# Rotated tiles turned by TensorE in transpose mode, preparation in smaller pieces, node sums on TensorE in the lead

## The reference

```
x = x + 0.5 * ffn(layernorm(x))      # 8 experts, threshold routing with capacity 1024
x = x + attention(layernorm(x))      # 16 heads of width 16, 4 nodes for each head
x = x + 0.5 * ffn(layernorm(x))
```

```
q, k, v = x @ Wq, x @ Wk, x @ Wv                    # 16 heads
node_probs = softmax(x @ Wr)                        # over the 4 nodes of each head
pos = clip(cumsum(node_probs, sequence) - node_probs, 0, 2047)
cos, sin = linear interpolation of the rotary tables at pos
cos_w, sin_w = sum over the nodes of node_probs * cos, node_probs * sin
q_r, k_r = q * cos_w + rotate_half(q) * sin_w, the same for k
scores = q_r @ k_r.T / 4 + log(node_probs @ node_probs.T + 1e-8), causal
out = softmax(scores) @ v, then @ Wo
```

## Time and profile before

| | us |
|---|---|
| median of three runs | 2959.88 |
| profiled execution | 2933.87 |
| its span | 2931.7 |
| TensorE matmul busy | 2448.4 (84%) |
| VectorE busy | 1713.1 (58%) |
| ScalarE busy | 1674.4 (57%) |
| GpSimd busy | 990.4 (34%) |

### The profile page before, as it was taken

One profiled execution on the slowest core, in us unless ns is written; L12 is line 12 of the kernel. 1 busy time (PEld: TensorE's weight loads), 2 busy tenths in 40 slices (PEclk: granted clock), 3 DMA queues, 4 the chain that ended last, 5 costly groups with the idle time before them and its releaser, 6 DMA issues. The chain is left out here.

```text
span 2931.7 us, 104032 instructions
## 1 busy us (share of the span) xinstructions
PE 2448.4 (84%) x45962; PEld 1906.9 (65%) x45964; DVE 1713.1 (58%) x3589; ACT 1674.4 (57%) x2102; POOL 990.4 (34%) x1423
## 2 busy tenths in 40 slices
PE   7287645577899999899999989999989999972875
PEld 4155412366688887778888768888778888741554
DVE  6733168888576568766566786666675111177331
ACT  6022123356677777667777767777766777560221
POOL 1078710244232224422222442322243222110787
PEclk9598866799999999999999999999999999985988
DMA  6455511121211112212112222111222111161555
GB/s 230 136 97 104 77 39 30 48 62 40 64 52 57 52 46 79 65 50 60 53 52 56 77 62 57 57 53 56 65 66 61 47 47 47 55 230 22 103 100 75
DMA packets 185107, 207.26 MB, mean 71 GB/s; under 512 B 35984, under 2 KB 151712, under 8 KB 184480
## 3 DMA queue, kind: packets, MB, share of 16 engines
q1 hardware_dynamic: 158880, 165.60, 19.0%
q0 software_dynamic: 24576, 34.10, 7.4%
q10 hardware_dynamic: 1152, 0.26, 0.0%
HBM read 131.68 MB, written 76.02 MB: 71 GB/s over the span
## 5 line engine op out<-in xcount | busy, mean ns | idle before, releaser
L1620 PEld LDWEIGHTS at_mix<-at_val,at_ew 128*64 128x64 f32 x34816 | 1223.5, 138 | 240.7 <-issue 36.1
L1204 ACT ACTIVATE at_ew<-at_ring 128x1024 f32<-128x1024 f32 (+1 forms) x1280 | 1125.2, 898 | 361.1 <-PE at_ring L1602 355.1
L1620 PE MATMUL at_mix<-at_val,at_ew 128*64 128x68 f32 x34816 | 1262.7, 224 | 45.0 <-DVE at_mixed L1466 30.1
L1602 PE MATMUL at_ring<-at_qT,at_kT 98*64 98x512 bf16 (+3 forms) x5120 | 698.7, 352 | 55.7 <-ACT at_ew L1204 36.2
L1125 POOL TENSOR_SCALAR_AFFINE_SELECT at_ew<-at_ew 128x256 f32<-128x256 f32 x512 | 292.6, 576 | 1078.2 <-ACT at_ew L1204 1077.2
L1466 DVE TENSOR_TENSOR at_mixed<-at_mix,at_prob 128x272 f32<-128x272 f32 x256 | 112.3, 439 | 437.1 <-PE at_mix L1620 435.7
L1602 PEld LDWEIGHTS at_ring<-at_qT,at_kT 98*64 98x64 bf16 x5120 | 228.7, 111 | 109.1 <-ACT at_ew L1204 48.3
L1147 POOL TENSOR_TENSOR at_val<-at_vo,at_val 128x256 f32<-128x256 f32 x384 | 266.6, 715 | 7.5
L328 POOL DMA_INDIRECT out_dram<-ffn_xn,ffn_idx_all x128 | 212.9, 1663 | 53.2 <-issue 34.1
L318 POOL DMA_INDIRECT ffn_xn<-table,ffn_idx_all x128 | 123.2, 963 | 311.8 <-DMA ffn_idx_all<-ffn_idx_hi 273.5
L1685 PE MATMUL at_side<-at_w_all,at_turned 128*64 128x512 f32 (+1 forms) x1024 | 203.2, 542 | 13.8 <-DVE at_bounded L1459 5.2
(11 more groups left out here) (224 smaller groups left out, 2759.8 us busy)
## 6 DMA issues: line engine op xcount, KB each, us to landing
table<-ffn_xn SPq DMA_DIRECT2D x32, 512.0 KB, 6.2
q_parts<-at_parts SPq DMA_DIRECT2D x64, 192.0 KB, 2.4
k_parts<-at_parts SPq DMA_DIRECT2D x64, 192.0 KB, 3.0
at_qT<-q_parts SPq DMA_DIRECT2D x128, 96.0 KB
at_kT<-k_parts SPq DMA_DIRECT2D x64, 192.0 KB
ffn_front<-in_L_attn_x_dram SPq DMA_DIRECT2D x16, 512.0 KB, 5.1
ffn_w_in<-in_L_ffn_w_dram SPq DMA_DIRECT2D x32, 256.0 KB, 3.6
at_xin<-out_dram SPq DMA_DIRECT2D x32, 256.0 KB, 5.9
```

What stands on the lines that cost most here:

```text
L1204: act.activation(ew[u % NE_BUF][:, a:b], ring[u % 2][:, a:b], ACT.Exp).then_inc(s["exp_ready"], 1)
L1602: lastm = pe.matmul(ring[u % 2][h:h + HALF, at:at + (CH - t) * P], kT[q][:, kc + j * P + h:kc + j * P + h + HALF], qT[q][:, qc + t * P:qc ...
L1620: m = pe.matmul(mix[block_of[u] % 2][h:h + HALF, t * K * VW:(t + 1) * K * VW], ew[u % NE_BUF][:, col + h:col + h + HALF], val[q][:, tile0 ...
```

## The change

- `turn_rotated` issues 8 matmuls of full width with `is_transpose=True` in place of 16 of half width.
- VectorE's steps are cut in smaller ones: `rotate` leaves its last two operations to `join_halves`; `positions` is split into `positions`, `whole_positions` and `first_angles`; `angles` gives its first two operations to `count_turns`; `node_products` is two steps. In a turn these stand at units of their own, each with its sums behind it, and `normalise` moves from unit 33 to 37 in long turns.
- ScalarE's `next_rsqrt` moves from unit 20 to 16 in short turns (29 to 25 in long ones), `trig` from 16 to 17 and `low_part` from 18 to 19 in short ones.
- In the lead VectorE shifts the logits and takes the softmax ahead of turn weights and rotation. For pairs 0 to 3 it doesn't sum the node products: TensorE does, in `sum_nodes` between `project_values` and `project_qk`, into `ring[0]`, and `turn_weights` reads the sums there. ScalarE's order in the lead stays.
- In the feed-forward programs several semaphores become counts of two common ones, and the residual copy counts on `rows_stored`, for which GpSimd waits ahead of its first gather.

```diff
-                pool.wait_ge(rows_stored, 16 * G + 16)
+                pool.wait_ge(rows_stored, 16 * G + (32 if residual else 16))
                 gather(0)
                 gather(1)
-                if residual:
-                    pool.wait_ge(residual_copied, 16)
...
-                SHORT_AT = (3, 6, None, 8, 9, 12, 15, 18, 16, 23, 20)
-                LONG_AT = (4, 6, 10, 8, 16, 18, 20, 23, BURST + 2, BURST + 4, BURST + 3)
+                SHORT_AT = (3, 6, None, 8, 9, 12, 15, 19, 17, 23, 16)
+                LONG_AT = (4, 6, 10, 8, 16, 18, 20, 23, BURST + 2, BURST + 4, BURST - 1)
...
-                def turn_weights():
+                def turn_weights(early=None):
+                    summed_nodes = sums[:, :, :]
+                    if early is not None:
+                        dve.wait_ge(s["sums_ps"], early + 1)
+                        summed_nodes = ring[0][:, :].rearrange("p (c n) -> p c n", c=4)
...
                 def lead(new, fin):
-                    if fin is not None:
-                        turn_weights()
-                        rotate(fin)
                     shift_logits(new)
                     node_softmax(new)
+                    if fin is not None:
+                        turn_weights(fin)
+                        rotate(fin)
+                        join_halves()
                     positions(new)
+                    whole_positions()
+                    first_angles(new)
                     statistics(new + 1)
+                    count_turns()
                     angles(new)
...
-                    node_products(new)
-                    node_sums(0)
-                    node_sums(2)
-
-                SHORT_AT = (0, 1, 6, 8, None, 10, 12, 13, 14, 18, 19, 20, 21, 23)
-                LONG_AT = (1, 2, 5, 8, 10, 14, 17, 20, 22, 30, 32, 25, 34, 33)
+                    for n in (0, 2):
+                        node_products(new, n, new < LEAD - 1)
+                    if new == LEAD - 1:
+                        for n in (0, 2):
+                            node_sums(n)
...
+                        if at == 1:
+                            turn_weights()
+                        if at == 2:
+                            rotate(fin)
+                        if at == (3 if short else 4):
+                            join_halves()
+                        if at == (14 if short else 20):
+                            largest_squares(fin)
+                        if at == (20 if short else 25):
+                            bound(fin)
...
+                        if at == (12 if short else 17):
+                            count_turns()
+                        if at == (13 if short else 18):
+                            angles(new)
+                        if at == (18 if short else 30):
+                            node_products(new, 0)
+                        if at == (19 if short else 32):
+                            node_sums(0)
+                        if at == (21 if short else 33):
+                            node_products(new, 2)
+                        if at == (22 if short else 35):
+                            node_sums(2)
+                    if more:
+                        if at == (15 if short else 22):
+                            statistics(new + 1)
+                        if at == (23 if short else 37):
+                            normalise(new + 1)
...
-                                    for h in range(0, P, HALF):
-                                        at = (g * 4 + n) * P + h
-                                        lastm = pe.matmul(side[h:h + HALF, n * GP + g * P:n * GP + (g + 1) * P],
-                                                          qkr[:, at:at + HALF], ident[:, :],
-                                                          start=(n % 2 == 0 and g == 0), stop=False, skip_group_check=True)
+                                    at = (g * 4 + n) * P
+                                    lastm = pe.matmul(side[:, n * GP + g * P:n * GP + (g + 1) * P], qkr[:, at:at + P], ident[:, :],
+                                                      is_transpose=True, start=(n % 2 == 0 and g == 0), stop=False, skip_group_check=True)
...
+                    turn_inputs()
+                    project_values()
+                    if fin is not None:
+                        sum_nodes(fin)
+                    for step in (project_qk, sums_before, turn_rotated, take_high_off, take_middle_off, turn_squares):
                         step()
+
+                def sum_nodes(t):
+
+                    pe.wait_ge(s["prods_ready"], t * 2 + 2)
+                    for n in range(2):
+                        each = prods[:, 2 * n:2 * n + 2, :].rearrange("p c (n k) -> p c n k", k=K)
+                        for k in range(K):
+                            lastm = pe.matmul(ring[0][:, n * 512:(n + 1) * 512], ident[:, :], each[:, :, :, k],
+                                              start=(k == 0), stop=(k == K - 1))
+                    lastm.then_inc(s["sums_ps"], 1)
```

More of the change, by code:

```diff
@@ L260, in _ @@
                 if residual:
-                    sp.dma_start(dst, src).then_inc(residual_copied, 16)
+                    sp.dma_start(dst, src).then_inc(rows_stored, 16)
                 def move_idx(e):
@@ L624, in _ @@
                 logits(G - 1)
-                pe.wait_ge(logits_ready, 1)
+                pe.wait_ge(act_stage, LOGITS_COPIED)
                 for t in range(GT):
@@ L1552, in unit @@
-                    if step == 3 and new is not None:
-                        node_softmax(new)
-                    if step == 4 and post is not None:
-                        add_residual(post, 0, 1)
-                    if step == 5 and new is not None:
-                        positions(new)
-                    if step == 6 and new is not None:
-                        angles(new)
-                    if step == 7 and fin is not None:
-                        largest_squares(fin)
-                    if step == 8 and more:
-                        statistics(new + 1)
@@ L1564, in unit @@
-                    if step == 9 and new is not None:
-                        node_products(new)
-                    if step == 10 and new is not None:
-                        node_sums(0)
-                    if step == 11 and fin is not None:
-                        bound(fin)
-                    if step == 12 and new is not None:
-                        node_sums(2)
-                    if step == 13 and more:
-                        normalise(new + 1)
+                    if fin is not None:
[9 more added lines that the diff above has]
+                            bound(fin)
```

86 lines of the change are left out of this document (47 added, 39 removed).

## The result

The changed kernel takes 3013.98 us, the median of four runs (3011.38 to 3017.36), beside 2960.14 us for the kernel before on the same chip: a ratio of 1.0186, 95% interval 1.0171 to 1.0200, or 54 us more. The prediction was 2961 us with a range of 2940 to 2988. It was wrong, and outside its range.

A forecast was written before the change was run, and what follows sets the result against it. TensorE was taken to bound the body, VectorE's chain the lead, and queue order the short turns. Terms +20.6 - 14.7 - 10.0 + 5.0 = +0.9 us on 2959.9 gave 2961 us, range 2940 to 2988.

The forecast's parts named there:

- The lead: Iterations before the first scores: node sums moved from VectorE to TensorE lengthen them, +20.6 us, bounds 15 and 48.
- The queue: Lead iteration: exponential behind the copy of qk, VectorE waiting for it before rotating; 38.6 us instead of 34.2.
- the 6.9 us for the 8 added matmuls: Lead, sum_nodes on TensorE: eight f32 matmuls at 0.86 us each, priced from contiguous reads.
- twice as long: Lead: upper bound of 48 us if the added matmuls on TensorE take double their priced time.
- The case: Lead: strided f32 reads at half speed, 13.8 us instead of 6.9 in four iterations, +27.6, total 2988; chance 0.10.
- The transposes: Rotated tiles in transpose mode: 0.7 us off each of 21 long turns, -14.7 us; short turns gain nothing.
- The long turns' pieces: VectorE's smaller steps in long turns remove two 5.3 us TensorE waits, -10 us, bounds -22 and +3.
- The short turns: ScalarE's and VectorE's new order there costs 1.3 us in each of four, +5 us, bounds -4 and +14.
- The two stalls: Short turns: waits for the variance at unit 16, then tables and sines at 17; +0.3 and +2.4 us, 1.1 regained.
- The forecast's rival: Short turns: TensorE's clock falls in two successive stalls, four turns cost 14 us instead of 5, total 2970; chance 0.26.
- The feed-forward: Both feed-forward stages: renamed semaphores cost nothing, the added residual-copy wait has over 10 us of cover; 0 us.
- The two slower rivals: Lead's strided reads at half speed, 2988, chance 0.10; short turns' two stalls with falling clock, 2970, chance 0.26.

The follow-up runs named there:

- The last experiment: The changed kernel with the lead of before and, in short turns, ScalarE's next_rsqrt back at unit 20, sines left at 17: 0.991 of the kernel before.

## Why the prediction was wrong

**The lead (+20.6 forecast, +47.8 in the trace).** The queue was right: `lexp` stands right behind the copy, VectorE idles ahead of it, and with adjoining reads the iteration is 38.8 to 40.6 where 38.6 was said. The term that failed is the 6.9 us for the 8 added matmuls, priced from rows that read adjoining values: it is 14.7, or 7.8 more in each of four iterations, 31 us; 27.2 were missing. The text named the lack and kept "twice as long" as its upper bound of 48, and the lead came out at that bound. That it met the bound to 0.2 us is in part luck: beside the forecast with the doubled price the first two iterations came out 2.5 and 1.8 us shorter, the last three 0.6 to 2.0 longer. The case had been given a chance of 0.10. With no row for strided reads and the price open between one and two times, the middle should have been in the sum and the double price in a good share of the chance. The rule of the Trainium skill, page "SBUF — State Buffer", section "Door 1: The DMA port swizzle", that each read in a new line of 16 bytes pays, is borne out by 14.74 against 7.13 us for the same instructions. It was the one statement about such reads that there was, and deserved more than a tenth.

**The transposes (-14.7 in the long turns).** Size right in the instruction (1.09 us), half right in the sum: 7.0 in the long turns, since ten of the 22 intervals gained nothing in sum, where the forecast had excepted three turns; 4.0 in the lead, which the sum held.

**The long turns' pieces (-10).** Wrong. The traced waits did shrink, 5.27 to 2.17 instead of the 1.3 expected. The false step was that the other VectorE stalls "have the same operations ahead of them in both orders": moving the angles from 17 to 18 put them next to the squares at 20, and a wait of 3.5 to 4.0 us came in all three later batches. Only the two longest waits of the old order had been walked through. And the root's move from 29 to 25 was priced at nothing in the long turns, where it stands behind about half of the 10.6 us that TensorE now waits on exponentials (1.5 before).

**The short turns (+5).** The two stalls were foreseen, their weights were not: +17.4, beyond the upper bound of 14. The text set the end of the statistics near 638.1, 28.8 us after the turn's inputs (609.3), and let TensorE start 0.3 us later than today, as if the wait for the variance only took the place of that for the sines; nearly all of its cost lay on the sines at 17. In the trace the statistics end 30.5 us after the inputs (699.6 and 669.1), TensorE starts 1.9 us later than before instead of 0.3, after waits of 5.9 on ScalarE and 5.5 on TensorE, and the sines behind it make a second one of 2.0. The last experiment turns the weights over: the root's place alone is worth 27.4 us over the four turns, and the sines at 17 cost nothing once the root is away. The forecast's rival had "two stalls in a row" for 14 us.

**The feed-forward (0).** Right as far as the runs can tell.

With the terms as measured (+47.8 for the lead, -7.0 for the transposes, 0 to +5 for the long turns' order, +17.4) the sum is +58 to +63, beside +60.7 in the traces and +54 in the medians. The two slower rivals were both true at once, and the body gave less than forecast. The prediction had named that pair, and left it out of its range with a chance of about 0.1: the range's upper end, 2988, is the price of the strided reads alone.

## What to carry to other kernels

A matmul's price is read from a row with the same access step: where the operand is read with a step that no row shows, put the high price into the sum. Before a reduction is moved to an idle engine, ask what is behind it there: here it took 4.67 us on VectorE beside TensorE's work, and at best 7.1 on TensorE, ahead of everything that stood behind it in the queue. And when an order is changed by hand, walk each step's new neighbours through all phases, not only the longest waits: the pieces cured the wait they aimed at and bought others. What decided in the turns was the place at which an engine meets a wait with others' work queued behind it, and a step moved in two tables has to be priced in both.

## What the runs showed of the hardware

- TensorE, f32, 512 moving columns with a step of 16 bytes: 14.74 us for sixteen records (eight matmuls) at a granted clock of 0.98 to 1.00, 7.13 us for adjoining values at 1.00, a factor of 2.07.
- VectorE, a product of 128x2048 f32: 2.29 us with adjoining values. Written with a step of 2 KB it takes 3.74; read with a step of 16 bytes and written in runs of 32 it takes 3.86:

```profile
442.67 3.86 DVE L1404 TENSOR_TENSOR at_prods<-at_cs,at_prob 128x2048 f32<-128x2048 f32 x1
```

  So the layout has to be paid for at one end or the other; both prices are under TensorE's. The Trainium skill, page "VectorE: DVE Perf Modes", section "Mode 1× (REGULAR) — the baseline", says that this mode gives one result a cycle and that odd strides work in it, and names no price for them; here such strides cost 1.6 to 1.7 times the time, and the measurement decides.
- A transpose of f32 in transpose mode leaves one record, and eight of 128x128 take 1.09 us where sixteen half-width matmuls took 1.91.
- TensorE's waits and its granted clock move together in the short turns: 0.93 over the second one before, 0.87 with the root at 16, 0.96 with the root at 20.
- The first feed-forward took from 376 to 390 us in traces of the same code: a difference of 10 us between single profiles says nothing of a change in another stage.
